# Loading one weight matrix for its absolute-value scan over two queues in place of one (attention and ternary FFN, 8 cores)

## The reference

```
q  = einsum('bse,hed->bhsd', x, Wq) + bq
kg = einsum('bse,ged->bgsd', x, Wk) + bk
vg = einsum('bse,ged->bgsd', x, Wv) + bv
attn = softmax(where(causal, -inf, q k^T / sqrt(128)))
x = layernorm(x + attn v)

ternary_quant(w): s = mean(abs(w)); clip(round(w / s), -1, 1) * s
g = silu(x w1q^T) * (x w3q^T)
x = layernorm(x + g w2q^T)
```

## Time and profile before

| | us |
|---|---|
| median of 2 runs | 2940.59 (2939.4 to 2941.79) |
| profiled execution, its own time | 2946.49 |
| its span on the slowest core (core 1) | 2944.8 |
| spans of the 8 cores | 2924.4 to 2944.8 |
| PE busy in the span | 1700.2 (58%) |
| ACT busy | 1110.6 (38%) |
| DVE busy | 810.4 (28%) |

### The profile page before, as it was taken

How to read it: one execution, slowest core, us unless ns; L and a number is a source line. 1 busy time by engine, 2 the same in 40 slices (tenths; PEclk the granted TensorE clock), 3 DMA queues, 4 the chain that set the end, 5 groups by cost and what they waited for, 6 DMA issues and landing times.

```text
span 2944.8 us, 19754 instructions; the slowest of 8 cores (2924.4 to 2944.8 us)
## 1 busy us (share of the span) xinstructions
PE 1700.2 (58%) x6824; PEld 717.9 (24%) x6824; DVE 810.4 (28%) x1243; ACT 1110.6 (38%) x1054; POOL 62.2 (2%) x120
## 2 busy tenths in 40 slices
PE   0392565534444444444233788888788757787780
PEld 0141222211111111111112333333333323333330
DVE  0020000222322222222365444444444430000004
ACT  0233200789988998989333000000000000101117
POOL 0000000000000000000000000000000000000000
PEclk9996777665565655566556999999999988888895
DMA  9848423354464454454404333333333332111102
GB/s 213 201 177 201 144 36 57 105 188 144 171 204 155 171 201 169 161 214 158 162 1 171 114 115 114 116 125 117 115 114 114 115 129 77 58 39 58 58 20 114
DMA packets 50743, 376.58 MB, mean 128 GB/s; under 512 B 5590, under 2 KB 5846, under 8 KB 16726
## 3 DMA queue, kind: packets, MB, share of 16 engines
q1 hardware_dynamic: 33558, 259.96, 25.2%
q0 software_dynamic: 17088, 115.35, 14.3%
HBM read 361.13 MB, written 39.32 MB: 136 GB/s over the span
## 4 chain that ended last, share of the span: by engine, by line
DMA 28%; PE 25%; ACT 17%; DVE 14%; issue 9%; another core or an unknown queue 4%; SPq 1%; DVEq 0%; ACTq 0%; POOL 0%; POOLq 0%
DMA af<-w_sb 19%; PE pH L923 11%; DVE ab L772 7%; ACT L489 6%; DMA ab<-wq_sb 5%; DVE ab L769 4%; ACT ab L489 3%; DMA ab<-w2qs 3%; ACT L374 2%; ACT af L374 2%; PE psR L320 1%; PE psB L320 1%; PE psO L320 1%; PE psA L320 1%
## 5 line engine op out<-in xcount | busy, mean ns | idle before, releaser
L809 PE MATMUL pH<-ab 128*128 128x512 bf16 x2752 | 641.1, 395 | 150.1 <-DVE ab L781 111.4
L457 PE MATMUL psR<-ab 128*128 128x512 bf16 (+3 forms) x384 | 151.5, 459 | 482.3 <-DVE ab L517 481.9
L489 ACT ACT_TABLE_LOAD x256 | 328.4, 1283 | 240.8 <-PE psA L436 201.2
L809 PEld LDWEIGHTS pH<-ab 128*128 128x128 bf16 x2752 | 273.6, 101 | 517.3 <-issue 229.2
L923 PE MATMUL pH<-ab 128*128 128x512 bf16 x1376 | 333.8, 409 | 103.2 <-DMA ab<-w2qs 103.2
L823 ACT ACTIVATE af<-pH,af 128x1024 f32<-128x1024 f32 x43 | 47.9, 1115 | 710.1 <-DVE ab L781 703.4
L769 DVE TENSOR_SCALAR ab<-af 128x2048 bf16<-128x2048 f32 x86 | 110.6, 1286 | 404.7 <-DMA af<-w_sb 404.7
L923 PEld LDWEIGHTS pH<-ab 128*128 128x128 bf16 x1376 | 141.7, 104 | 291.5 <-issue 152.4
L517 DVE TENSOR_TENSOR ab<-ab 128x128 bf16<-128x128 bf16 x256 | 56.5, 223 | 543.5 <-ACT ab L489 543.4
L772 DVE SCALAR_TENSOR_TENSOR ab<-af,ab 128x2048 bf16<-128x2048 f32 x86 | 202.2, 2352 | 9.0
L457 PEld LDWEIGHTS psR<-ab 128*128 128x128 bf16 x384 | 33.6, 107 | 620.4 <-issue 619.4
(11 more groups left out here) (101 smaller groups left out, 1334.8 us busy)
## 6 DMA issues: line engine op xcount, KB each, us to landing
af<-w_sb POOLq DMA_DIRECT2D x86, 1024.0 KB, 5.8
af<-w_sb SPq DMA_DIRECT2D x86, 1024.0 KB, 4.9
af<-w_sb SPq DMA_DIRECT2D x16, 2752.0 KB, 11.5
af<-w_sb SPq DMA_DIRECT2D x64, 688.0 KB, 12.2
w2qs<-ab SPq DMA_DIRECT2D x16, 1376.0 KB, 5.6
ab<-w2qs SPq DMA_DIRECT2D x16, 1376.0 KB, 6.0
ab<-xkvT POOLq DMA_DIRECT2D x8, 1024.0 KB, 51.1
ab<-wq_sb POOLq DMA_DIRECT2D x16, 512.0 KB, 5.2
```

The source lines that it names most:

```text
L457: tensor.matmul(psR[:, b2 * 512:b2 * 512 + n2], ones128, abf(A_PT + OFF[kc] + b2 * 512, n2), start=(kc == 0), stop=stop)
L489: INC(scalar.activation(abf(A_PT + OFF[kc], N), ps[:, 0:N], AF.Exp, bias=m16col), "ex", 1)
L809: last = tensor.matmul(ps[:, b2 * 512:(b2 + 1) * 512], lhs, abf(A_XKV + ec * 1024 + b2 * 512, 512), start=(ec == 0), stop=(ec == NEC - 1))
```

## The change

The loads of w2 for the scan are split between two issuing engines. The odd pieces stay with SP on semaphore `ld`. The even pieces are issued by ACT on its own queue, on a new semaphore `ls`: the first at the very start of ACT's stream, the others after ACT has finished the even piece before in the same buffer. Each buffer has its own semaphore now, so ACT waits before piece i for piece i alone. The loads, their number, sizes and buffers, and the ACTIVATEs stay as they are.

```
+        def p_abs_sync(sync):
             W(sync, "ld", LD_CONSTS)
+            for i in range(1, NEC, 2):
+                if i >= 3:
+                    W(sync, "fS", i - 1)
+                ph1_ld[i] = INC(sync.dma_start(out=aff(F_ABS + 6144, HIDP),
+                                               in_=d_w2[i]), "ld", 16)
+        on("sync", p_abs_sync)
+
+        def p_abs_scalar(scalar):
+            INC(scalar.dma_start(out=aff(F_ABS, HIDP), in_=d_w2[0]), "ls", 16)
             for i in range(NEC):
-                if i >= 2:
-                    W(sync, "fS", i - 1)
-                INC(sync.dma_start(out=aff(F_ABS + (i % 2) * 6144, HIDP),
-                                   in_=d_w2[i]), "ld", 16)
-        on("sync", p_abs_sync)
-
-        for i in range(NEC):
-            def sfun(scalar, i=i):
-                W(scalar, "ld", LD_CONSTS + 16 * min(i + 2, NEC))
+                if i % 2 == 0:
+                    W(scalar, "ls", 16 * (i // 2 + 1))
+                else:
+                    W(scalar, "ld", ph1_ld[i])
                 buf = aff(F_ABS + (i % 2) * 6144, HIDP)
                 INC(scalar.activation(buf, buf, AF.Abs,
                                       accum_out=aff(F_PAR + i, 1)), "fS", 1)
-            on("scalar", sfun)
+                if i % 2 == 0 and i + 2 < NEC:
+                    W(scalar, "fS", i + 1)
+                    INC(scalar.dma_start(out=aff(F_ABS, HIDP),
+                                         in_=d_w2[i + 2]), "ls", 16)
+        on("scalar", p_abs_scalar)
```

More of the change, by code:

```diff
@@ L106, in _build_nc @@
         sems = {}
-        for name in ["ld", "lg", "la", "lb", "st", "lc", "fT", "fS", "fV",
+        for name in ["ld", "lg", "la", "lb", "st", "lc", "ls", "fT", "fS", "fV",
                      "sc", "ex", "mk", "av", "rev", "rc", "oev",
@@ L338, in _build_nc @@
         NAB2 = len(ab2_pieces)
+        ph1_ld = {}
         def p_abs_sync(sync):
             W(sync, "ld", LD_CONSTS)
-            for i in range(NEC):
-                if i >= 2:
-                    W(sync, "fS", i - 1)
-                INC(sync.dma_start(out=aff(F_ABS + (i % 2) * 6144, HIDP),
-                                   in_=d_w2[i]), "ld", 16)
-        on("sync", p_abs_sync)
-        for i in range(NEC):
-            def sfun(scalar, i=i):
-                W(scalar, "ld", LD_CONSTS + 16 * min(i + 2, NEC))
+            for i in range(1, NEC, 2):
[6 more added lines that the diff above has]
+            INC(scalar.dma_start(out=aff(F_ABS, HIDP), in_=d_w2[0]), "ls", 16)
+            for i in range(NEC):
+                if i % 2 == 0:
+                    W(scalar, "ls", 16 * (i // 2 + 1))
+                else:
+                    W(scalar, "ld", ph1_ld[i])
                 buf = aff(F_ABS + (i % 2) * 6144, HIDP)
```

## The result

The changed kernel takes 2958.2 us in the median of 43 runs, the kernel before 2945.0 in the median of 42 beside it. The ratio is 1.0058, with a 95% interval from 1.0037 to 1.0080: slower by 0.6%, or some 17 us. The medians are of all runs, but in some of them the cores of a die ran at a lower clock and took some per cent longer, and the ratio leaves those out. The time is inside the range of 2952 to 3000, with the forecast sign, at half of the forecast +34: the interval reaches to +24, and the forecast +34 lies outside it.

What follows compares the result with a forecast made beforehand. The prediction took PE to wait for POOL's loads on full DMA engines, with nobody waiting for the w2 scan. Its terms, 64 - 19 - 11 = +34 us, gave 2975 us on a 2940.6 us basis; range 2952 to 3000.

Steps and rivals of the forecast that it cites:

- forecast +34: Whole kernel: the predicted net slowdown in us, the sum of 64 - 19 - 11.
- account of the DMA engines: Before PE's start: engines full without slack, so what w2 gets POOL loses; one w2 piece costs 8.3 us.
- Part one: K/V loads before PE's first K matmul: more w2 traffic delays that start from 123.3 to 187 us, +64 us.
- turn for each queue: DMA sharing while w2 loads: each queue gets a turn, leaving POOL 1/3 beside both halves, 1/2 beside one.
- rival of a shared turn: Before PE's start: both hardware queues share one turn, POOL keeps half; PE starts at 164, 2952 us; chance 0.20.
- starved case: Before PE's start: POOL's turn falls to a quarter or less; PE starts at 216, 3003 us; chance 0.10.
- Part two: Wait for xqT and two wq before the Q projection: shortened from 52.4 to 33.5 us, -19 us.
- Part three: First wq loads in the Q projection: free of w2 traffic, each takes 5.1 us, -11 us together.
- What was costed at nothing: ACT's 8 DMA issues, under 5.5 us within idle time, and w2 traffic beside K and V: no cost.
- case of a gain without a loss: Before PE's start: POOL's loads lose nothing, start stays 123, only 30 us of gain remain, 2911 us; chance 0.05.
- that of nothing moving: Before PE's start: w2 traffic keeps its pace as if issued from one engine, 2940 us; chance 0.05.

Runs made afterwards that it cites:

- e9: Kernel after, ACT's first load held until the constants land and the old wait on two pieces restored, two queues kept; PE starts at 123.2 us, ratio 1.0012.
- e10: Kernel after, with ACT's first w2 load waiting until the constants have landed; PE starts at 148.7 us, ratio 1.0041.
- e1: Kernel after, but SP issues all 16 w2 loads from one queue, ACT still waiting for its own piece alone; PE starts at 174.2 us, ratio 1.0075.
- e3: Kernel after, with both halves of the scan held until POOL's K/V loads have landed; PE starts at 84.1 us, ratio 0.9872.
- e5: Kernel before, with SP's first scan load held until POOL's ten K/V loads have landed; PE starts at 82.5 us, ratio 0.9894.
- e6: Kernel after, scan held until the K/V loads land, and from piece 12 until xqT and two wq land; PE starts at 82.2 us, ratio 0.9904.
- e4: Kernel before, with ACT's 16 ACTIVATEs of the scan in one function instead of 16; ratio 0.9973.
- e7: Kernel before, with ACT's attention stream in one function instead of 342; 2811.2 us, ratio 0.9598.

## Why the prediction was right, and where it was off

**The account of the DMA engines held.** Until PE starts the DMA engines are full, and T is what POOL's loads and the constants need (83 us) plus 8.3 us for each piece of w2 served until then. The share of q1 and q10, less 3.4 for the constants and over 8.3, gives the pieces:

| | w2 pieces by T | 83 + 8.3 x pieces | T measured |
|---|---|---|---|
| before, core 1 | 4.8 | 123 | 123.3 |
| e9, core 3 | 4.9 | 124 | 123.7 |
| e10, core 4 | 7.9 | 149 | 148.4 |
| after, core 1 | 9.2 | 159 | 159.9 |
| e1, core 4 | 10.8 | 173 | 173.6 |
| e3, core 0 | 0 | 83 | 84.8 |

With the engines full, the T worked out must come near the T measured, since the pieces are themselves taken from shares of T. What is tested is that POOL's part stays the same and that w2's bytes give the same pieces: they give 4.8, 5.0, 8.1, 9.0 and 10.7 for the first five rows, and T within 2.2 us. And where no piece was served, T was 84.1, 82.5 and 82.2 (e3, e5, e6).

**Part one, +64, was mis-sized: +36.6.** The step that failed is the rate of w2, 8.3 of every 14.6 us from 2 us on, which made 12.5 pieces by T; 9.2 were served, and 3.3 x 8.3 are the 27 us. Of it, one cause is plain: I took SP's half to begin at 19 us, but the early load pushed the constants, and it began at 36.5. So only three pieces were done when ACT started its third pass, at 64. The other is the pace: 6 passes between 59.4 and 157.6, 16.4 us each and not 14.6. The first two loops took 30.8 and 28.6 us, near the forecast 29.2, but by luck: w2 had more than two thirds while both halves loaded, and ACT's passes fell together where I had each within the load of the other. The third took 38.8 us, in good part beside wv, whose rows are the longest (32 KB): from 145 to 155 us 57 packets of POOL had 56.8% of the engines, and 57 of ACT's queue 33.5%. An error in the rate is more than doubled in T, since a later T lets more pieces in: T = (83 - 1) / (1 - 0.57), and 1 / 0.43 is 2.3.

**The turn for each queue was half right.** While both halves loaded, POOL had 27% (a third was forecast). But the reading that gave it, that two pieces in one queue get no more than half, was wrong: one queue had 58.8% from 24 to 50 us in the kernel before and has 58% in e1. The rival of a shared turn came out near in number: its T of 164 is closer to the measured 160 than my 187, and its 2952 us closer to 2958 than my 2975. So that the time fell into the range is luck in part, since the range was stretched down to that rival. Its mechanism is refuted by the same 27%, as it had POOL at half. That the second queue was the cause, which I took for granted in all rivals, is refuted by e9 and e1: the new wait is. Packets explain both: 140 to 136 in e1, and 105, 103 and 94 of the three queues from 71 to 88 us. There a packet of POOL took 27.1% of 17 x 16 us over 105 = 0.70 us and one of SP 1.0, and one for one makes POOL's share 0.70 / 2.70 = 26%. I had set strict turns by packets aside for the 290 to 400 of the earlier trace rows, but the surplus of POOL there lies at the two ends of the window, where w2 had little or nothing in flight; between them it is 251 to 248. The Trainium skill, DMA: Bandwidth & Descriptors, section "Queues, rings and completion order", has that rule, and these three stretches agree with it.

**Part two, -19, was right:** -16.8 here, -17.4 in e6 (52.9 to 35.5). **Part three, -11, came to -4.2.** The wq loads gave back 8.4 (PE's waits for wq sum to 144.0 us before and 118.8 after; less the first, 52.9 and 36.1, that is 91.1 and 82.7), but PE's matmuls took 4.2 us more, which the forecast left out; the clock of the stage was 0.78 and not 0.79, and whether that is all of it no run shows.

**What was costed at nothing cost nothing:** ACT's issues took 0.33 to 0.41 us each, and K and V ran at their old pace beside the heavier traffic. I had not seen in the order of the instructions that 15 branches of ACT go and with them 15 table loads. With them the pause of a buffer is 7.2 us and not 8.5, and my sum would have given a T some 6 us later still. The scan ended at 235 us and not near 225. The case of a gain without a loss (T of 123) and that of nothing moving fell with T; the starved case (T of 216) did not come about, though its condition nearly did: POOL had 27% beside xkvT and 20.0% beside wk (100 to 117 us) while both halves loaded. But in each loop ACT's passes left POOL alone for a while, and SP's half began late.

## What to carry to other kernels

A load that nobody waits for isn't free while another is waited for: count the full DMA engines as an account, and each piece of background work served before the awaited load has landed moves its landing by that piece's service time. So look at what a removed wait had been holding back; here the clumsy wait on two pieces was a throttle, and to hold the background scan behind the awaited loads (e5) is worth more than to speed it up. And count the table loads of ACT in the profile: where they repeat with the same functions, join the blocks (e7).

## What the runs showed of the hardware

- One queue that was never empty took 58% of the DMA engines against POOL's 42% (22 KB rows against 16 KB; e1, and the kernel before from 24 to 50 us), and 67% against 34% beside the 8 KB rows of wk (e1, 111 to 122 us), about one packet for one in both.
- The masks (0.5 MB) landed 34.1 us after their issue with w2's first piece beside them, 16.5 before.
- A second issuing queue changed neither T nor the time while the old wait stood (e9); with the wait on the own piece it made T 26 us smaller (e10 against e1).
- An ACT table load of 1.28 us came with each new block of ACT's stream, also where the same function stood in the block before: 16 to 1 (e4), and in attention 342 to 1 (e7), with Exp, Copy and Abs mixed in that block.
